# Second layers of experts 0 to 3 and 4 to 7 pairwise together on TensorE, with a new order on VectorE and GpSimd: a one-core vision tower step

## The reference, cut to what matters

```python
h = einsum('bnk,dk->bnd', patches(x), W) + b                  # embedding
h = h + scan(tanh(xp_t + h_prev @ W_hh.T))                    # over the 16 images
x = layernorm(h)
gate = x @ gate_w + gate_b;  top 2 of 16, softmax of the two
hid = relu(einsum('bsh,ehf->bsef', x, w1) + b1)               # first layer, 64 -> 128
out_e = einsum('bsef,efh->bseh', hid, w2) + b2                # second layer, 128 -> 64
y = x + sum of the two chosen, weighted
out = h + layernorm(y) * gamma + beta
```

## Time and profile before

| | us |
|---|---|
| median of 3 runs | 514.97 |
| lowest and highest | 513.32, 515.25 |
| the profiled execution, its own time | 513.06 |
| its span, first to last instruction | 511.0 |
| PE busy | 493.3 |
| DVE busy | 447.3 |
| ACT busy | 342.9 |
| POOL busy | 183.2 |
| granted TensorE clock, mean | 0.987 |

### The profile page before, as it was taken

One profiled execution on the slowest core, in us unless ns is written; L12 is line 12 of the kernel. 1 busy time (PEld: TensorE's weight loads), 2 busy tenths in 40 slices (PEclk: granted clock), 3 DMA queues, 4 the chain that ended last, 5 costly groups with the idle time before them and its releaser, 6 DMA issues.

```text
span 511.0 us, 8780 instructions
## 1 busy us (share of the span) xinstructions
PE 493.3 (97%) x2980; PEld 324.1 (63%) x2980; DVE 447.3 (88%) x881; ACT 342.9 (67%) x586; POOL 183.2 (36%) x137
## 2 busy tenths in 40 slices
PE   8789999999999999999999999999999999999993
PEld 5465666666666666666766666666666666666652
DVE  1678888989989898998989999898989899999775
ACT  1556675868677695857668586767858676665652
POOL 3220304436152443616144262515335362223133
PEclk9989999999999999999999999999999999999997
DMA  6229193957639192775819395483919366481911
GB/s 145 75 67 226 35 221 82 199 126 167 162 80 228 49 223 79 160 168 113 196 36 221 96 195 130 104 205 84 232 38 216 94 135 159 117 196 47 227 40 31
DMA packets 31067, 69.04 MB, mean 135 GB/s; under 512 B 6720, under 2 KB 10800, under 8 KB 30896
## 3 DMA queue, kind: packets, MB, share of 16 engines
q1 hardware_dynamic: 31024, 68.49, 57.9%
HBM read 60.39 MB, written 8.08 MB: 134 GB/s over the span
## 4 chain that ended last, share of the span: by engine, by line
PE 90%; DVE 2%; issue 2%; DMA 1%; ACT 1%; SPq 1%; POOL 1%; POOLq 0%; DVEq 0%; ACTq 0%
PE pZ L911 38%; PE pO L928 35%; PE pA L863 3%; PE pA L830 2%; PE pA L853 2%; PE pA L880 2%; PE pA L942 2%; DMA gbias<-gate_b 1%; PE pB L892 1%; PE pA L843 1%; PE pB L942 1%; PE pB L880 1%; PE pA L854 1%; DVE prod L679 1%; PE pO L802 0%
## 5 line engine op out<-in xcount | busy, mean ns | idle before, releaser
L503 ACT ACTIVATE hexp<-pZ,b1c 128x784 f32<-128x784 f32 x256 | 221.5, 912 | 108.9 <-PE pZ L911 108.9
L928 PE MATMUL pO<-hexp,w2s 128*64 128x392 f32 x1024 | 198.5, 503 | 0.6 <-ACT hexp L503 0.3
L911 PE MATMUL pZ<-xt,w1hi 128*128 128x392 f32 x512 | 187.8, 367 | 1.4 <-ACT xt L431 1.4
L679 DVE SCALAR_TENSOR_TENSOR prod<-pO,b2c,spread 128x392 f32<-128x392 f32 x256 | 149.8, 620 | 31.8 <-PE pO L928 30.3
L911 PE MATMUL pZ<-xt,w1lo 128*128 128x392 f32 x512 | 173.8, 340 | 0.0
L911 PEld LDWEIGHTS pZ<-xt,w1hi 128*128 128x128 f32 x512 | 96.1, 188 | 46.9 <-issue 18.3
L366 POOL TENSOR_TENSOR inv_std<-var,nhalf 112x7 f32<-112x7 f32 x48 | 82.5, 1727 | 105.3 <-DVE var L569 105.3
L928 PEld LDWEIGHTS pO<-hexp,w2s 128*64 128x64 f32 x1024 | 70.2, 136 | 75.3 <-issue 62.2
L695 DVE TENSOR_TENSOR acc<-acc,prod 128x784 f32<-128x784 f32 x111 | 111.3, 1002 | 0.1
L911 PEld LDWEIGHTS pZ<-xt,w1lo 128*128 128x128 f32 x512 | 96.4, 188 | 0.0
L379 POOL TENSOR_TENSOR h2b<-h2c,bet 112x448 f32<-112x448 f32 x15 | 18.4, 1226 | 162.3 <-DMA h2c<-h_dram 162.3
(11 more groups left out here) (114 smaller groups left out, 503.3 us busy)
## 6 DMA issues: line engine op xcount, KB each, us to landing
spread<-gates_dram SPq DMA_DIRECT2D x126, 392.0 KB, 8.9
h_dram<-h SPq DMA_DIRECT2D x16, 248.1 KB, 2.4
h2c<-h_dram SPq DMA_DIRECT2D x16, 248.1 KB, 9.0
out<-yo SPq DMA_DIRECT2D x15, 196.0 KB, 9.1
xcur<-x_in SPq DMA_DIRECT2D x16, 112.0 KB, 7.8
xcur<-x_in SPq DMA_DIRECT2D x16, 84.0 KB, 8.9
w1f<-w SPq DMA_DIRECT2D x2, 512.0 KB, 5.8
spread<-gates_dram SPq DMA_DIRECT2D x4, 196.0 KB, 3.6
```

The costliest lines, as they stand in the source:

```text
L503: nc.scalar.activation(hexp[u % RING][:, :].rearrange("p (b c) -> p b c", b=2), halves(pZ[u % 2]), ACT.Relu, bias=b1c[:, u:u + 1]).then_in ...
L679: nc.vector.scalar_tensor_tensor(out=prod[q % RING][:, b * HALF:(b + 1) * HALF], in0=halves(pO)[:, b, :], scalar=b2c[:, q:q + 1], in1=spre ...
L911: last = nc.tensor.matmul(halves(pZ[e % 2])[:, b, :], w[:, e, :], xt[par][:, b * HALF:(b + 1) * HALF], start=(k == 0), stop=(k == 1))
L928: last = nc.tensor.matmul(halves(pO)[k * D:(k + 1) * D, b, :], w2s[:, e, :], hexp[e % RING][:, b * HALF:(b + 1) * HALF], start=True, stop= ...
```

## The change

On PE, second layers 0 and 1 now both stand after first layers 2 and 3 (and embed_turn), and second layers 2 and 3 both after first layers 6 and 7; hidden_turn is issued between 2 and 3. Layers 4 to 7 keep their places, and so do recur, embed_in, gates_turn and sum_turn. On DVE the step is written as one list: product 1 follows product 0 at once, the two adds that were due come after them, product 3 follows add_state, and the adds 0, 1 and 2 stand behind gate_weights. On POOL `close_out` of image t-2 is done in step t (before: image t-1 in step t), held until half of second layer 0 is there, and `add_beta` is held until half of second layer 2 is there. On ACT `close_norm` moves from behind relu 15 to behind relu 1 of the next step; square_h2, square_h1 and exp_gap move by one expert. SP stores image t-2 behind the load of h2.

```diff
+        def second_layers_at(u):
+
+            return {3: (0, 1), 7: (2, 3), 11: (4,), 13: (5,), 15: (6,)}.get(u, ())
...
             def fetch_h2(s):
+                if not known(s, 1):
+                    sp.wait_ge(h2b_set, 2 * s)
...
                 if close:
                     fetch_h2(t - 1)
+                if close and not known(t, 2):
+                    store(t - 2)
...
                 pool.wait_ge(h2_loaded, 16 * s + 16)
+                if not known(s, 1):
+                    CLOSE.wait(pool, s - 1, "out")
...
+                if close and not known(t, 2):
+                    pool.wait_ge(y_ready, 2 * t * Q + 1)
+                    close_out(t - 2)
                 if close:
+                    pool.wait_ge(y_ready, 2 * (t * Q + 2) + 1)
                     add_beta(t - 1)
                 if embed:
                     bias_h1(t + 3, 1 - par)
                 if mix:
                     rstd(MIX, t + 2, 1)
-                if close:
-                    rstd(CLOSE, t - 1, 2)
                 if embed:
                     rstd(EMBED, t + 3, 0)
                 if close:
-                    close_out(t - 1)
+                    rstd(CLOSE, t - 1, 2)
...
+                    if close and u == 1 and not known(t, 2):
+                        close_norm(t - 2)
                     if gate and u == at(t, 1, first=7):
                         keep_xt(t + 1, 1 - par)
...
-                    if gate and u == at(t, 6, first=8):
+                    if gate and u == at(t, 7, first=8):
                         exp_gap(t + 1)
...
-                    if mix and u == at(t, 9, first=11):
+                    if mix and u == at(t, 8, first=11):
                         square_h2(t + 2)
+                    if embed and u == 12:
+                        square_h1(t + 3, 1 - par)
...
-                    if close and u == 15:
-                        close_norm(t - 1)
...
-                for u in range(E):
-                    if experts and u % 2 == 1:
-                        if u > 1:
-                            product(t, u // 2 - 1, par)
...
+                if mix and not known(t, 1):
+                    scale_h1(s, par)
+                if experts and not known(t, 1):
+                    product(t - 1, Q - 1, 1 - par)
+                if gate and not known(t, 1):
+                    bias_logits(g)
+                    find_first(g)
+                product(t, 0, par)
+                product(t, 1, par)
...
+                    add(t - 1, Q - 2, 1 - par)
+                    add(t - 1, Q - 1, 1 - par)
+                if gate:
+                    find_second(g)
+                product(t, 2, par)
+                if mix:
+                    add_state(s, par)
+                product(t, 3, par)
+                if gate:
+                    gate_weights(g)
+                add(t, 0, par)
+                add(t, 1, par)
+                add(t, 2, par)
+                product(t, 4, par)
+                if mix:
+                    norm_var(MIX, s, 1)
+                add(t, 3, par)
+                if close:
+                    close_center(c)
+                product(t, 5, par)
+                if embed:
+                    norm_var(EMBED, a, 0)
+                if mix:
+                    norm_scale(MIX, s, 1, x2[:, :, :], h2[:, :, 0:D])
+                add(t, 4, par)
+                if close:
+                    norm_var(CLOSE, c, 2)
+                product(t, 6, par)
+                if mix:
+                    low_part(s)
+                add(t, 5, par)
...
-                    if experts and u % 2 == 1:
-                        if u > 1:
-                            second_layer(t, u // 2 - 1)
-                        elif not known(t, 1):
+                    if experts:
+                        if u == 1 and not known(t, 1):
                             second_layer(t - 1, Q - 1)
-                    if mix and u == at(t, 7, first=9):
-                        hidden_turn(t + 2)
+                        for q in second_layers_at(u):
+                            second_layer(t, q)
+                            if mix and q == 2:
+                                hidden_turn(t + 2)
```

More of the change, by code:

```diff
@@ L312, in body @@
                 if known(STEPS - 1 - t, 1):
-                    sp.wait_ge(h2b_set, 2 * t)
                     fetch_h2(t)
-                if close:
                     store(t - 1)
@@ L413, in _ @@
             run(pool, body)
+            close_out(STEPS - 2)
             rstd(LAST, 0, 2)
@@ L521, in body @@
                         keep_gt(t + 1)
-                    if mix and u == at(t, 9, first=11):
+                    if mix and u == at(t, 8, first=11):
                         square_h2(t + 2)
+                    if embed and u == 12:
+                        square_h1(t + 3, 1 - par)
                     if close and u == 13:
                         square(CLOSE, t - 1, "center", 2, cen[:, :, :])
-                    if embed and u == 13:
-                        square_h1(t + 3, 1 - par)
                     if known(t, 1) and u == 4:
@@ L559, in _ @@
             run(act, body)
+            close_norm(STEPS - 2)
             CLOSE.wait(act, STEPS - 2, "norm")
@@ L698, in body @@
                 g, s, a, c = t + 1, t + 2, t + 3, t - 1
-                for u in range(E):
-                    if experts and u % 2 == 1:
-                        if u > 1:
-                            product(t, u // 2 - 1, par)
-                        elif not known(t, 1):
-                            product(t - 1, Q - 1, 1 - par)
-                    if close and u == 13:
-                        norm_var(CLOSE, c, 2)
-                    if experts and u % 2 == 1:
-                        if u > 3:
-                            add(t, u // 2 - 2, par)
-                        elif not known(t, 1):
-                            add(t - 1, Q - 2 + u // 2, 1 - par)
-                    if mix and u == 0 and not known(t, 1):
-                        scale_h1(s, par)
-                    if known(t, 1) and u == 3:
-                        norm_scale(MIX, g, 1, x2[:, :, :], h2[:, :, 0:D])
-                    if known(t, 1) and u == 5:
-                        low_part(g)
-                    if gate and u == at(t, 1, first=4):
-                        bias_logits(g)
-                        find_first(g)
-                    if mix and u == at(t, 7, first=9):
-                        add_state(s, par)
-                    if gate and u == at(t, 3, first=6):
-                        find_second(g)
-                    if gate and u == at(t, 7, first=9):
-                        gate_weights(g)
-                    if mix and u == 11:
-                        norm_var(MIX, s, 1)
-                    if close and u == 12:
-                        close_center(c)
-                    if embed and u == 14:
-                        norm_var(EMBED, a, 0)
-                    if mix and u == 13:
-                        norm_scale(MIX, s, 1, x2[:, :, :], h2[:, :, 0:D])
-                    if mix and u == 15:
-                        low_part(s)
@@ new lines, in body @@
+                if mix and not known(t, 1):
[7 more added lines that the diff above has]
+                product(t, 1, par)
+                if known(t, 1):
+                    norm_scale(MIX, g, 1, x2[:, :, :], h2[:, :, 0:D])
+                    low_part(g)
+                    bias_logits(g)
+                    find_first(g)
+                else:
+                    add(t - 1, Q - 2, 1 - par)
+                    add(t - 1, Q - 1, 1 - par)
```

## The result

The change makes the kernel 2.4% slower: 526.67 us (median of 4, 525.94 to 529.15) against 515.04 (4 runs), ratio 1.0239, 95% interval 1.0203 to 1.0274. The forecast was 525.5, within 518 to 531.5.

A forecast was written before the change was run, and what follows sets the result against it. PE, packed at 29.48 us a step, was taken to bound the kernel. Steps 1 to 12 add 6.7 us and the ends 4.8, together 11.5; between 524.6 and 526.5, by base, 525.5 was forecast, range 518 to 531.5.

The forecast's parts named there:

- What bounds: Twelve steps: PE is packed, 29.48 us a step of its own work; what DVE saves there is worth nothing.
- The seam: Second layers 0 to 1 on single buffer pO: 1.80 us between starts instead of 1.46, 0.34 more, released by DVE.
- The rival without a wait: Second layers 0 to 1: PE writes on without waiting for DVE, 1.34 us; no change, 516.5 us; chance 0.10.
- recur by itself: recur between first layers loses the neighbour of its own array shape: 0.12 us more a step.
- hidden_turn: Between second layers 2 and 3 it covers the wait: 2.4 us against 1.80 needed, no cost; without it 0.34.
- embed_turn: On PE, waiting for keep_xt behind close_norm on ACT: late by 0.1 us a step, bounds 0 and 0.5.
- DVE's order: DVE before product 0: ready 0.2 to 0.3 us ahead, with scale_h1 at 0.62 us instead of 1.56.
- its rival: DVE late at second layer 0, adds or gate_weights perhaps slowed beside POOL: seam 2.5 us, time 533.5; chance 0.16.
- The steps: Steps 1 to 12: each 0.34 + 0.12 + 0.1 = 0.56 us longer, 6.7 us in all.
- The ends: Steps 13 to 15: 1.5 us more each, from bare seams and first layers in runs of four; with step 0, 4.8.
- Step 0: First step, with its own order: 0.3 us more, a guess between -0.7 and 1.5.
- The sum: Whole kernel: 6.7 + 4.8 = 11.5 us more; 524.6 on base 513.06, 526.5 on the median 514.97, forecast 525.5.

The follow-up runs named there:

- experiment 11: The changed kernel with hidden_turn behind second layer 3 and DVE's product 3 ahead of add_state: 531.64 us, ratio 1.0344.
- experiment 10: The changed kernel with PE's order of before, close_norm behind relu 3, product 1 straight behind the two adds, product 3 behind gate_weights: 515.65 us, ratio 1.0035.
- experiments 4 and 8: 4: the kernel before with the pairs on PE alone, 545.38 us; 8: the changed kernel without POOL's two waits for second layers 0 and 2, 542.87 us.
- experiment 9: The kernel before with second layer 0 moved behind first layer 5, so that recur stands between second layers 0 and 1: 515.59 us, ratio 1.0031.
- experiment 7: The changed kernel with close_norm behind relu 3 and keep_xn1t on ACT instead of behind relu 1: 527.35 us, ratio 1.0245.
- experiment 6: The changed kernel with embed_turn between second layers 0 and 1 instead of ahead of them: 535.08 us, ratio 1.0405.

## Why the prediction was right

**What bounds.** Right. PE is packed in before, and DVE's freed 3.9 us brought nothing.

**The seam.** Right: 1.79 and 1.80 for 1.80. It is shown three times: in the change, at layers 2 and 3 in experiment 11 (0.33 a step), and by its absence in experiment 10. The rival without a wait falls, since the seams carry the release by DVE's product, and where that comes late (experiments 4 and 8) layer 1 comes late with it.

**recur by itself.** Somewhat more than said: 0.89 to 0.90 and 1.47, 2.37, for 2.21, that is 0.16 and not 0.12. The Trainium skill, TensorEngine Tiling (Array Packing), section Tiling Modes, says that a mode change drains TensorE. The prediction's "agree in size" compares rows with rows alone; rows agree with the page in sign (0.15 for one stretch fewer in experiment 9), and there the gain was lost to places around it, so by that rule alone the order is not to be chosen.

**hidden_turn.** Right: 2.40 to layer 3, and 0.33 a step when it is taken away.

**embed_turn.** Right in size: late by 0 to 0.32, in the mean of the twelve steps 0.10, where I had 0.1 and bounds of 0 to 0.5; it also takes 0.02 longer. The cause of the upper value is the one named, a late rstd: in the step shown relu 1 ends at 250.68, and close_norm starts only as POOL ends at 250.78.

**DVE's order.** Right in its verdict. The margin of 0.2 to 0.3 us is 0.19 to 0.26 in seven of the twelve steps and 0.08 to 0.09 in four, so thinner than said in a third of them. scale_h1 went from 1.56 to 0.62. That POOL held back no longer slows DVE holds for scale_h1 and find_first alone. One add a step carries it now, 1.90 us beside bias_h1 where an add without POOL takes 0.97; the prediction had named that neighbour under its rival and priced it at nothing in the sum. It brings product 4 to 1.37 us behind its layer (269.90 to 271.27) and PE doesn't wait. The Trainium skill, SBUF — State Buffer, section Who interferes with whom, has a VectorE operation with two SBUF inputs and a GpSimd operation that reads SBUF exclude each other; the trace agrees, and the products, which read `pO`, keep 609 to 629 ns throughout.

**The steps.** 0.56 said, 0.63 measured: 0.33 seam, 0.16 recur, 0.12 embed_turn. Twelve: 7.55 for 6.7.

**The ends.** 4.5 said for steps 13 to 15, 4.1 measured: 1.5 for 1.5 in step 13, and 2.6 for 3.0 behind it, where before had a wait of its own (first layers 6 and 7 of step 14 take 1.97 there). The runs of four take 3.62 to 3.72 for 3.7, and 4.09 in step 13. Step 0: 0.3 said; experiment 7 has, at before's clock, 0.9 more at the end of step 0, 0.25 of it already there at the first x2_turn, so 0.65, its own run of four at 3.79 being the largest part.

**The sum.** 11.5 said, 11.6 between the medians (526.67 - 515.04). An agreement to 0.1 is luck: the three parts measured in single executions make 7.55 + 4.1 + 0.65 = 12.3, and single executions of the changed kernel lie 3 us apart. The base was chosen between 513.06 and 514.97, and the 1.2 us by which the forecast is short are that choice.

What stays open: why h2 lands early enough in some steps of experiment 7 and not in others, and whether the four thin margins and the late embed_turn of the same steps come from one late rstd. Neither was taken apart.

## What to carry to other kernels

Two writers of one PSUM buffer can't start closer together than the reader's start, its first read and the release (here 1.03 + 0.62 + 0.15 = 1.80 us); the first writer's own 1.47 covers part of it, and something of 0.33 us or more between them covers the rest (recur, embed_turn and hidden_turn each did). Count that from a place in the trace where the two already meet, and any edit that separates work elsewhere must not be charged with what it saves. A wait is priced by what is queued behind it on its engine (0.33 us a step or 1.4, for the same edit), and a run of producers by the number of buffers behind it. Undoing an edit in a kernel whose other engines were re-ordered for it doesn't give its price: take the new waits away too, or compare with a second variant that has them.

## What was unexpected of the hardware

DVE and POOL side by side on SBUF: a DVE operation of 0.28 us doesn't take twice its time but about as long as POOL's whole operation beside it (1.05 and 1.17 us, POOL's 1.14 and 1.13). In experiment 6 that adds 1.67 us to two operations of find_first, and in experiment 7 1.47 us to two adds (3.51 for 2.04), where POOL's own second operation went from 1.14 to 1.76. Two adds in a row into the same `acc` cost more than two apart without any POOL: the second starts 0.10 us after the end of the first, in all 48 such pairs of the changed kernel, where an add behind a product starts 0.08 us before the product's end. Holding POOL back by two waits was worth 16 us of 527. And filling a slot where PE had only a shape change to lose (experiment 9) moved a step by 0.10 us in the wrong direction.
